# Rotary products taken from PSUM, and the split of q and k moved to GpSimd in attention

## The reference, cut to what matters

```python
q = ln(x) @ Wq;  kv = ln(x) @ Wkv            # 256 -> 256 each, 16 heads of 16
t = t * cos(freqs) + rotate_half(t) * sin(freqs)   # for q and for kv
att  = einsum('bmd,bnd->bmn', q * 16**-0.5, kv)
out  = softmax(att) @ kv                      # kv is both key and value
x = x + out @ Wout + bout
```

## Time and profile before

| | us |
|---|---|
| median of 3 runs | 2205.71 (2195.53 to 2214.84) |
| profiled execution, its time | 2201.75 |
| its span | 2199.9 |

### The profile page before, as it was taken

The page is one execution under the profiler, slowest core; times in us unless marked ns, Lnnn a source line. Parts: engine busy times, 40 slices in busy tenths (PEclk is TensorE's granted clock), DMA queues, the critical chain, the costliest instruction groups (busy, mean ns, idle before and its releaser), DMA issues. The chain is left out here.

```text
span 2199.9 us, 53264 instructions
## 1 busy us (share of the span) xinstructions
PE 1983.9 (90%) x16620; PEld 1028.0 (47%) x16620; DVE 1922.4 (87%) x3093; ACT 1481.1 (67%) x2778; POOL 648.7 (29%) x895
## 2 busy tenths in 40 slices
PE   6777589999999999999999999999999139999998
PEld 3333233333333333333333333333477128999997
DVE  7888879999999999999999999999477778888863
ACT  3444168888888888888888888888744014554443
POOL 7888301110110111011011101101187015555653
PEclk9999679999999999999999999999999559999999
DMA  2666733332332233233233323323476023343432
GB/s 88 221 219 213 188 93 88 86 80 72 86 84 74 80 86 79 72 86 84 74 80 86 79 72 86 84 74 82 149 260 237 17 93 88 88 92 83 106 66 27
DMA packets 167627, 225.58 MB, mean 103 GB/s; under 512 B 52116, under 2 KB 120055, under 8 KB 167543
## 3 DMA queue, kind: packets, MB, share of 16 engines
q1 hardware_dynamic: 146790, 198.86, 31.6%
q0 software_dynamic: 12288, 17.05, 4.6%
q10 hardware_dynamic: 8464, 8.67, 1.2%
HBM read 130.35 MB, written 94.09 MB: 102 GB/s over the span
## 5 line engine op out<-in xcount | busy, mean ns | idle before, releaser
L774 DVE TENSOR_REDUCE a_mx<-a_sm 128x2 f32<-128x1024 f32 x1024 | 1233.9, 1221 | 53.0 <-PE a_sm L727 36.5
L861 ACT ACTIVATE a_prob<-a_st 128x512 f32<-128x512 f32 x2048 | 1112.7, 597 | 206.2 <-PE a_st L696 174.1
L696 PE MATMUL a_st<-a_q,a_k 50*128 50x512 f32 x2048 | 757.6, 451 | 14.1 <-DMA a_q<-a_mrow 13.4
L727 PE MATMUL a_sm<-a_k,a_q 48*128 48x512 f32 x2048 | 756.4, 458 | 10.0 <-DVE a_mx L774 8.4
L714 PE MATMUL a_pv<-a_prob,a_v 128*32 128x256 f32 x8192 | 656.8, 392 | 22.8 <-ACT a_oraw L868 19.9
L696 PEld LDWEIGHTS a_st<-a_q,a_k 50*128 50x128 f32 x2048 | 306.9, 186 | 438.3 <-ACT a_prob L861 417.8
L714 PEld LDWEIGHTS a_pv<-a_prob,a_v 128*32 128x32 f32 x8192 | 161.8, 108 | 406.7 <-ACT a_prob L861 212.5
L727 PEld LDWEIGHTS a_sm<-a_k,a_q 48*128 48x128 f32 x2048 | 300.4, 188 | 22.1 <-DVE a_mx L774 20.1
L836 POOL TENSOR_TENSOR a_v<-a_v_raw,a_zero 128x256 f32<-128x256 f32 x64 | 39.6, 620 | 667.5 <-PE a_pv L714 667.5
L1776 ACT ACTIVATE e_hT<-e_ps_h,e_b1b 128x512 f32<-128x512 f32 x128 | 88.3, 690 | 204.0 <-PE e_ps_h L1813 200.1
L826 POOL TENSOR_TENSOR a_nsplit<-a_nm,a_zero 128x16 fp32r<-128x16 f32 x64 | 14.4, 226 | 501.3 <-DVE a_nm L782 501.3
(11 more groups left out here) (144 smaller groups left out, 2363.2 us busy)
## 6 DMA issues: line engine op xcount, KB each, us to landing
qkv_parts<-p_parts SPq DMA_DIRECT2D x64, 512.0 KB
a_q<-qkv_parts SPq DMA_DIRECT2D x128, 128.0 KB, 2.8
a_k<-qkv_parts SPq DMA_DIRECT2D x128, 128.0 KB, 3.0
attended<-a_oraw SPq DMA_DIRECT2D x64, 256.0 KB, 2.1
e_w<-in_fc_dram SPq DMA_DIRECT2D x16, 1024.0 KB, 5.4
token_table<-f_tab ACTq DMA_DIRECT2D x8, 1056.0 KB, 7.8
p_x<-in_x_dram SPq DMA_DIRECT2D x16, 512.0 KB, 8.0
values<-p_values SPq DMA_DIRECT2D x8, 1024.0 KB, 20.0
```

Of the source, the lines that this page charges most:

```text
L696: nc.tensor.matmul(st[:, slot % RING], kb[rows, q.buf, jt * P:(jt + 1) * P], qb[rows, q.buf, ic * CHUNK:(ic + 1) * CHUNK], start=True, sto ...
L727: mm = nc.tensor.matmul(sm[:, slot, h], qb[rows, q.buf, qt * P:(qt + 1) * P], kb[rows, q.buf, kc * CHUNK:(kc + 1) * CHUNK], start=True, st ...
L774: nc.vector.tensor_reduce(mx[:, qt, kc, :], sm[:, slot], AX.X, ALU.max, negate=True).then_inc(max_done, 1)
L861: nc.scalar.activation(prob[:, jt % 2, h, ic * CHUNK:(ic + 1) * CHUNK], st[:, slot % RING], ACT.Exp, scale=DH ** -0.5).then_inc(drained, 1)
```

## The change

In the projection, the x tile is only centred ahead of its transpose, by ScalarE (mean - x, `centre`), and 1/sqrt(var + eps) is applied later: DVE's `products` reads the projected tile straight from PSUM and multiplies it by rstd and by -cos (one operation of 512 columns), and by rstd and the sin table (two operations of 256). The copy `qkv` is gone. GpSimd makes the whole sum of 512 columns. The turned result is stored once, not split (`turned`, four transfers a sequence in place of eight). The loops are straight code now, and the loads of pairs 0, 1 and 2 are spread over passes 1, 2 and 3 of SP.

In attention, SP's `load` brings the unsplit q and k of a pair by broadcast into three row blocks of one buffer `raw` (single), three pairs ahead, and stands in SP's body behind the fetch of the reciprocals and ahead of `put_maxima`. GpSimd makes the blocks: `take_high` multiplies raw by a mask with 1 in the low block's rows and rounds to fp32r; `cut` subtracts that from raw into `a_q`, `a_k`, so the rows with mask 1 get the low part and the others the high part. Each is done for k and q and for two halves of 512 columns: eight operations of 128 x 512 a pair. In the body of pair q they are made for pair q+2, behind `place` and `scale`. For pairs 0 and 1 they are made during the projection (`cut_early`). The load of a next pair waits until the last one is cut; TensorE waits for all four cuts of a pair ahead of its first maxima matmul.

```diff
 def load(sp, q):
     if not (q.p is not None and q.p < 3):
-        sp.wait_ge(filled, (q.n - 2) * FILLS)
         sp.wait_ge(v_placed, q.n - 2)
     sp.dma_start(v_raw[:, q.buf] ...).then_inc(v_in[q.buf], 16)
-    for h in range(2):
-        for kind, (buf, runs) in enumerate(((qb, Q_RUNS), (kb, K_RUNS))):
-            for row, part, parts in runs:
-                ...
-                sp.dma_start(buf[row:row + parts * DH, q.buf, :] ...).then_inc(qk_in[q.buf], 16)
+    if not q.first():
+        sp.wait_ge(cut_done, CUT_OPS * q.n)
+    for kind in (1, 0):
+        for h in range(2):
+            sp.dma_start(raw[head_rows(h, DATA_ROWS), kind],
+                         raw_dram[bass.ds(q.n * 2 + h, 1), kind].to_broadcast([DATA_ROWS // DH, DH, N])
+                         ).then_inc(raw_in, 16)
...
+def take_high(pool, q, kind, half):
+    cols = slice(half * CHUNK, (half + 1) * CHUNK)
+    pool.wait_ge(raw_in, 16 * RAW_LOADS * (q.n + 1))
+    nc.gpsimd.tensor_tensor(high[:, kind, cols], raw[:, kind, cols],
+                            mask[:, kind:kind + 1].to_broadcast([P, CHUNK]), ALU.mult).then_inc(high_done, 1)
+
+def cut(pool, q, kind, half):
+    cols = slice(half * CHUNK, (half + 1) * CHUNK)
+    pool.wait_ge(high_done, CUT_OPS * (q.n + 1) if kind == 0 else CUT_OPS * q.n + HALVES)
+    if not (q.p is not None and q.p < 3):
+        pool.wait_ge(filled, (q.n - 2) * FILLS)
+    nc.gpsimd.tensor_tensor((qb, kb)[kind][:, q.buf, cols], raw[:, kind, cols], high[:, kind, cols],
+                            ALU.subtract).then_inc(cut_done, 1)
...
 # SP's body
-            elif q.plus(2).exists():
-                load(sp, q.plus(2))
...
             if q.follows(2):
                 fetch_rden(sp, q.plus(-2))
+            if q.plus(3).exists():
+                load(sp, q.plus(3))
             if q.plus(1).exists():
                 put_maxima(sp, q.plus(1))
...
 # TensorE's maxima
             if v == 0 and h == 1:
-                pe.wait_ge(qk_in[q.buf], (q.turn + 1) * 16 * QK_LOADS)
+                pe.wait_ge(cut_done, CUT_OPS * (q.n + 1))
...
 # GpSimd's body
             split(q)
+            pool.wait_ge(turned, q.n + 1)
             if not q.first() and q.plus(2).exists():
                 place(q.plus(2))
             if q.follows(3):
                 scale(pool, q.plus(-3))
+            if q.plus(2).exists():
+                for kind in (1, 0):
+                    for half in range(HALVES):
+                        take_high(pool, q.plus(2), kind, half)
+                for kind in (1, 0):
+                    for half in range(HALVES):
+                        cut(pool, q.plus(2), kind, half)
...
 # VectorE in the projection, in place of normalise, cos_product, first_sum and low_part
+        def products(it, k, n):
+            i = k % TILES
+            dve.wait_ge(q_done, n + 1)
+            dve.wait_ge(rstd_done, n // GROUP + 1)
+            ...
+            nc.vector.scalar_tensor_tensor(out=t_cos[:, k % 2]..., in0=ps_q[:, k % 2]..., scalar=rstd[:, k:k + 1],
+                                           in1=cosb[:, i:i + 1, :]..., op0=ALU.mult, op1=ALU.mult)
+            for h in range(2):
+                nc.vector.scalar_tensor_tensor(out=to[:, :, h * HALF:(h + 1) * HALF], in0=src[...], 
+                                               scalar=rstd[:, k:k + 1], in1=sinb[...], op0=ALU.mult, op1=ALU.mult)
...
 # SP in the projection, body of a pass
             load(it + 1, 0)
             if past(it):
+                sp.wait_ge(raw_out[0], 16 * 4)
+                sp.wait_ge(v_out[0], 16)
+                load_first(sp, it - 1)
                 store(it - 1, 1)
```

More of the change, by code:

```diff
@@ L282, in vector, with body @@
+        def body(j):
+            n = tile(j, 0)
+            if n:
+                statistics(*n)
+            n = tile(j, ROT)
+            if n:
+                products(*n)
         nc.vector.memset(mhalf[:], -0.5).then_inc(halves_set, 1)
@@ L284, in vector, with gpsimd @@
         dve.wait_ge(consts_in, 64)
-        flow.run(dve, body, CUT)
-    def gpsimd(pool):
+        steps(body, ROT)
+    def gpsimd(pool, between):
         def inverse_root(it, k, n):
@@ L316, in turn, with body, centre @@
                 pool.wait_ge(values_done, n - 1)
[L317 to L326 removed]
+            nc.gpsimd.tensor_tensor(rot[:, k % 2], t_cos[:, k % 2], t_sin[:, k % 2], ALU.add).then_inc(rot_done, 1)
+        def body(j):
+            n = tile(j, SUM)
+            if n:
+                sums(*n)
+            n = tile(j, 0)
+            if n and j % GROUP == GROUP - 1:
+                inverse_root(*n)
+            between(pool, j)
         pool.wait_ge(consts_in, 64)
         pool.wait_ge(halves_set, 2)
[L330 removed]
+        steps(body, SUM)
     def scalar(act):
+        def centre(it, k, n):
+            act.wait_ge(mv_done, n - n % GROUP + GROUP)
+            if past(n, 2):
+                act.wait_ge(xT_done, n - 1)
+            nc.scalar.activation(xc[:, k % 2], xb[:, k], ACT.Identity, bias=mv[:, k, 0:1], scale=-1.0
+                                 ).then_inc(xc_done, 1)
         def turned_tokens(it, k, n):
@@ L392, in turn_back, with body @@
             mm.then_inc(rT_done, 1)
-        def body(it, j):
-            for stage, lag in ((turn_tokens, NORM), (products, PROJ), (turn_back, BACK)):
-                tile = flow.at(it, j, lag)
-                if tile:
-                    stage(*tile)
+        def body(j):
+            for stage, lag in ((turn_tokens, TURN), (products, PROJ), (turn_back, BACK)):
+                n = tile(j, lag)
+                if n:
+                    stage(*n)
         pe.wait_ge(consts_in, 64)
-        flow.run(pe, body, BACK)
+        steps(body, BACK)
     return Stage(sync, tensor, vector, scalar, gpsimd), stored, banks_free
@@ L430, in attend @@
     kb = a.sb("a_k", [P, 3, N], F32R)
-    ones = a.sb("a_ones", [CUTS, P])
+    mask = a.sb("a_mask", [P, 2])
     v_raw = a.sb("a_v_raw", [P, 3, TILES, 2, DH])
@@ L814, in set_buffers @@
         nc.gpsimd.memset(vb[:], 1.0).then_inc(set_up, 1)
-        nc.gpsimd.memset(ones[:], 1.0).then_inc(set_up, 1)
+        nc.gpsimd.memset(raw[:], 1.0).then_inc(set_up, 1)
     def gpsimd(pool):
@@ L1954, in constants @@
     group = i // DH
+    row = i % HEAD_ROWS // DH
     return {
         "ident": np.eye(P, dtype=np.float32),
-        "rot_cos": by_tile(np.concatenate([cos, cos], -1)),
-        "rot_sin": by_tile(np.concatenate([-sin, sin], -1)),
+        "rot_cos": by_tile(np.concatenate([-cos, -cos], -1)),
+        "rot_sin": by_tile(np.concatenate([sin, -sin], -1)),
+        "split_mask": np.stack([row == low for low in LOW_ROWS], 1).astype(np.float32),
         "same": (group[:, None] == group[None]).astype(np.float32),
```

234 lines of the change are left out of this document (94 added, 140 removed).

## The result

| kernel | median us | runs | ratio to before |
|---|---|---|---|
| before | 2204.58 (2195.53 to 2214.84) | 4 | |
| after | 2937.31 (2920.95 to 2945.63) | 4 | 1.331 [1.326, 1.337] |

What follows compares the result with a forecast made beforehand. PE and DVE, both full in attention, were taken as the bound. From 2202 us, less 42 for the projection, plus 310 for waits and clock (5.0 us a pair), plus 4, came 2474, given as 2475; range 2300 to 2660.

Steps and rivals of the forecast that it cites:

- What bounds the kernel now: Attention: PE (98%) and DVE (97%) are both full; no engine is full in the projection.
- The new GpSimd chain: Attention: eight operations take 9.24 us, end at T0 + 11.1, and PE waits 3.4 us a pair, 211 us in all.
- T0: Attention: the instant GpSimd places the values of pair q+2, when PE has finished the last values of pair q-1.
- the ninth step: Attention: TensorE's first maxima matmul of pair q+2, ninth of sixteen steps, at T0 + 7.68, where it waits for the cuts.
- Rival (b): Attention: the cuts are hidden, needing eight operations under 5.85 us; only the projection's gain is left, 2164 us; chance 7%.
- The change on SP: SP's queue in attention: the maxima rows just fit behind the loads; costed at nothing, at most 1 us a pair (62 us).
- rival (c): Attention: load ahead of put_maxima makes the maxima rows late, 5.16 us a pair over now, 2484 us; chance 8%.
- What the clock does: Attention: the gap drops TensorE's clock in three pairs of four, 5 us a spell, costing 1.6 us a pair.
- Rival (a): Attention: the clock holds and the gap costs only the wait, 2375 us, with bounds 2290 to 2440; chance 25%.
- rival (d): Attention: the lower clock lasts most of each pair, 28.7 us a pair, 2681 us and more, bounded near 2750; chance 12%.
- The change in the projection: Projection: less engine work a tile, 2.9 us instead of 3.55, gains 42 us, bounds 10 to 80.
- The sign: Whole kernel: slower 0.91, faster 0.07, same 0.02.

Runs made afterwards that it cites:

- rows: The changed kernel with each pair's raw loads as twelve plain transfers of 16 rows instead of four broadcasts: 2684.61 and 2729.68 us.
- before_wait5: The kernel before the change, with five useless 128 x 512 GpSimd additions behind place and scale that PE waits for: 2207.07 us, ratio 1.001.
- before_wait9: The kernel before the change, with nine useless 128 x 512 GpSimd additions behind place and scale that PE waits for: 2840.8 us, ratio 1.288.
- wait9_fill: before_wait9 with 24 useless maxima matmuls on TensorE ahead of its wait for the GpSimd additions: 2520.31 and 2575.01 us.
- fixed_late: The changed kernel with 16-row loads, cuts ahead of place and scale, load ahead of put_on, early cuts six steps later: 2185.26 us, ratio 0.990.
- rows_fill: rows with 16 useless maxima matmuls on TensorE ahead of its wait for the cuts in every pair: 2572.55 and 2617.21 us.
- early: The changed kernel with only GpSimd's cutting operations moved ahead of place and scale: 2711.16 us, ratio 1.229.
- fixed2: fixed_late with SP's fetch of the reciprocals moved behind max_rows: 2126.49 us, ratio 0.964.

## Why the prediction was wrong

**What bounds the kernel now** was right: PE and DVE full, nothing to spare in attention, so every late step is paid for in full.

**The new GpSimd chain** was right, term by term, as far as the instants go: take_high 1.01 us (1.05 forecast), cut 1.26 (1.26), end at T0 + 10.8 (11.1), the wait at the ninth step up to 2.7 us (3.4); it is shorter (1.3 at 1026 us) or absent where PE does the first eight steps in part at the lower level, so that rows lost 143 us by it in place of 211. Rival (b) is ruled out: eight operations take 9.0 us where 5.85 would have done, and five of them (before_wait5) are indeed free.

**The change on SP, costed at nothing, is the first step that failed.** I had counted the bytes ("about as many") and the issues, from a_rrep, and added 2 us of landing; nothing was allowed for a transfer that is itself slow. (The old kernel has nine loads a pair with that of the values, the new one five; "eight" left that one out.) The issues took 3.56 us for four, a little over the 2.0 to 3.4 taken. But the loads then moved for some 12 us, and the put of the maxima landed after 10.8 us instead of 1.4. This is rival (c), whose landing of 3 us was 10.8; it cost 217 us of waiting, and 208 to 253 us in all by rows against after: the waits of both kinds fall from 267 to 143 us, and the time at the lower level in attention from 1355 to 1021. Why the broadcast is slow is a matter of its shape, since rows moves the same bytes with 16 rows in each transfer and lands each in 2.2 us. In after, 0.20 to 0.22 of the DMA engines' time was used in 1029 to 1040 us, and three of sixteen would be 0.19. The Trainium skill (DMA: Bandwidth & Descriptors, Rules for kernel authors) states just this: a transfer is spread over at most as many of the 16 engines as its outermost dimension counts, and it names a leading broadcast of few copies as the case to avoid. Here the outermost count is 3. By that rule the loads run on 3 engines; the trace agrees, with three packets at a time in after and up to 16 in rows, whose outermost count is 16. Only these two shapes were run, and the records don't name the engine of a packet. The rule was at hand and should have been rival (c)'s price.

**What the clock does is the second step that failed, and the larger.** The fall behind the gap was forecast, the price of it mis-sized: "5 us for a spell, nearer to the short ones", 1.6 us a pair or 99 us in all. PE's busy time grew by 528. Measured means are 24 us (after), 18 (rows), 19 (before_wait9). Of the two rows that I had for the length of a spell, I leaned on the projection's (3.4 us) and used the one with attention's own mix (15.5 us) as a far bound. With it taken, and the fall in three pairs of four, the sum is the forecast's own upper bound, 2681; with a fall in every pair it is 2202 - 42 + 62 x (3.4 + 0.43 x 15.5) + 4 = 2788. rows, the kernel that has this wait alone, took 2685 and 2730. The clock records of before also show that the 15.5 us were only the end of a stretch at the lower level, which had begun at 235.6 us, 46 us ahead of the first scores. The chance of a fall was too low: in rows and before_wait9 every gap had one (56 of 56, 53 of 53), and pairs without a fall had no gap. The projection had suggested less, rightly for itself: there, the gap of 2.66 us ahead of 199 us has none. In before_wait9 a gap of at most 4.0 us costs 633 / 62 = 10.2 us a pair.

**The rivals on the clock.** Rival (a), that the clock holds, had 25% and is ruled out: wait9_fill shows that PE's rest is what brings the fall. The sum beside rival (a) doesn't follow: with the bounds of chain and projection its terms give 2281 to 2586, not 2290 to 2440. The bound "near 2750" of rival (d) held in rows, with one wait. It broke in after, where the wait for the maxima rows comes on top; and it wouldn't hold for one longer wait either, as before_wait9, whose chain ends 1 us later, takes 2841, or 2795 less the projection's 46. What (d) said of the mechanism came true: the wait for the cuts shrinks, to 50 us in after, as the ninth step comes late. The gaps of the two kinds mostly don't meet in one spell, though: only 12 of the 68 began while the clock was still low.

**The change in the projection** was right in its number, in part by luck: the first scores came 46 us earlier (42 forecast). But the tiles themselves ended at 205.4 us in place of 239.4, 34 us earlier (PE's last transposes had been put near 197); the other 12 are the wait ahead of the first scores, 1.67 us in place of 13.43, which I had set against the early cuts. DVE's product of 512 from PSUM took 0.75 us (0.68 taken), GpSimd's sum 1.27 (1.26). That the early cuts would wait ahead of GpSimd's sums was named, and happened: 32.7 us in two waits. Put behind, they give back another 32 (first scores of fixed_late at 202.6 us).

**The sign** was right with 0.91; the range was too narrow at its upper end: rows, with one wait alone, lies above its 2660 already, and (c) and (d) were taken as alternatives where they add up.

What stays open: why the clock comes back so late in attention (18 to 24 us in the mean), with PE working steadily at the lower level all the while; and how the remainder in rows_fill divides.

## What to carry to other kernels

Find the instant at which the consumer asks for what a new producer makes, and the one at which the producer ends: here everything hung on T0 + 7.7 against T0 + 10.8, and moving the same work ahead of two small operations took that wait away (early), and with loads that land in time made it free (fixed2). When PE is the bound, price a gap by the clock behind it, with the spell read from a stretch of the same mix of work, not only by its own length. And before a transfer is put into a queue, ask what stands behind it, and look at the outermost dimension of its shape: here three copies moved three packets at a time, and what was small and urgent behind them landed late.

## What the runs showed of the hardware

- A 2.63 us rest of TensorE in a loop of 20 us, otherwise 98% busy, was followed by 13 us at the 1.2 GHz level (rows), and by 18 to 24 us in the mean of three kernels (after, rows, before_wait9). Gaps of about 1 us had none in 47 cases of 57 (wait9_fill). Filling 3.2 of the 4.2 us with useless matmuls made the kernel 266 to 320 us faster.
- In attention no spell in any of these kernels begins without such a gap; before, before_wait5 and fixed2 have neither a gap of 1 us there nor a spell, once the first one is over.
- The fall can come after work has been taken up again: at 1034.8 us, 2.0 us behind the end of the gap (rows).
- Four broadcast loads with 3 outermost copies, 192 KB each by the view, moved at 65 to 85 GB/s with 0.20 to 0.22 of the DMA engines' time, three packets of 4096 bytes at a time, and a 16 KB transfer behind them took 10.8 us to land; as 16-row loads, with up to 16 packets at a time, 2.2 and 1.7 us.
- GpSimd on 128 x 512: 1.01 us with a repeated second operand, 1.26 with two dense ones. Adding a short row of zeros to itself, read again and again, took 1.04 us (before_wait9, mean of 558), and 1.11 from one to the next (9.97 / 9), each waiting for the one before.
